# Decoder layer on one core: score operands projected already turned and read back from DRAM by pairs, and the feed-forward products of the first sequence put at the head of each attention step of the second

## What is computed

```python
q, k, v = split(x @ w_qkv)                      # 256 -> 3 x 256
q = q * cos + rotate_half(q) * sin              # the same for k
att = softmax(where(causal, q @ k.T * DH**-0.5, min))
x = layernorm(x + (att @ v) @ w_proj)
q = x @ Wq.T + bq; k = ctx @ Wk.T + bk; v = ctx @ Wv.T + bv
x = layernorm(x + softmax(where(mask, q @ k.T / 4, -inf)) @ v @ Wo.T + bo)
h = silu((x @ w1.T) * s1) * ((x @ w2.T) * s2)   # 256 -> 1024, ternary weights
h = gelu((h @ h1.T) * s3); h = gelu((h @ h2.T) * s4)   # 1024 -> 1024
x = layernorm(x + (h @ w3.T) * s5)              # 1024 -> 256
```

## Time and profile before

| | us |
|---|---|
| median of 3 runs | 994.16 |
| lowest and highest | 990.64, 994.91 |
| the profiled execution: its own time | 994.44 |
| the profiled execution: span of the instructions | 992.7 |
| busy in the span: TensorE (PE) | 869.8 |
| VectorE (DVE) | 559.3 |
| ScalarE (ACT) | 376.6 |
| GpSimd (POOL) | 363.5 |
| mean granted TensorE clock | 0.924 of full |

### The profile page before, as it was taken

The page is one execution under the profiler, slowest core; times in us unless marked ns, Lnnn a source line. Parts: engine busy times, 40 slices in busy tenths (PEclk is TensorE's granted clock), DMA queues, the critical chain, the costliest instruction groups (busy, mean ns, idle before and its releaser), DMA issues.

```text
span 992.7 us, 13083 instructions
## 1 busy us (share of the span) xinstructions
PE 869.8 (88%) x4466; PEld 553.7 (56%) x4466; DVE 559.3 (56%) x1422; ACT 376.6 (38%) x788; POOL 363.5 (37%) x575
## 2 busy tenths in 40 slices
PE   5879999797889877979999878889889869999997
PEld 2544444335725455645454435468765457888886
DVE  4697888777677654675565654342553476116213
ACT  0315665562453122224555664522343433112210
POOL 4312323546254332052222244252433375335433
PEclk9957999769867898979999989999999999999999
DMA  9909101002002111210101202133211126000000
GB/s 311 323 3 401 45 2 44 23 1 78 4 3 85 48 59 64 86 43 23 44 23 44 85 2 65 42 128 107 65 31 59 71 81 252 1 1 22 1 1 23
DMA packets 24955, 69.37 MB, mean 70 GB/s; under 512 B 4539, under 2 KB 12680, under 8 KB 24712
## 3 DMA queue, kind: packets, MB, share of 16 engines
q1 hardware_dynamic: 24888, 68.50, 20.1%
HBM read 65.87 MB, written 13.63 MB: 80 GB/s over the span
## 4 chain that ended last, share of the span: by engine, by line
PE 73%; DVE 12%; POOL 5%; ACT 5%; issue 3%; DMA 1%; SPq 0%; POOLq 0%; DVEq 0%; ACTq 0%
PE bank L880 13%; PE bank L946 11%; PE bank L684 8%; PE bank L701 7%; PE bank L649 5%; PE bank L635 3%; PE bank L584 3%; PE bank L867 3%; DVE bank L1300 3%; PE bank L928 2%; PE bank L823 2%; DVE max_raw L1298 2%; PE bank L811 2%; ACT prob_s L1103 2%; PE bank L734 1%
## 5 line engine op out<-in xcount | busy, mean ns | idle before, releaser
L1103 ACT ACTIVATE prob_s<-bank 128x512 f32<-128x512 f32 (+3 forms) x384 | 166.4, 494 | 131.3 <-PE bank L684 129.0
L1633 POOL TENSOR_SCALAR_AFFINE_SELECT prob_s<-prob_s 128x128 f32<-128x128 f32 x256 | 83.9, 343 | 178.4 <-ACT prob_s L1103 175.9
L1300 DVE CUSTOM_DVE_ANT_0 bank<-bank,causal_bf 128x128 f32<-128x128 f32 (+3 forms) x256 | 122.4, 511 | 46.0 <-PE bank L649 44.5
L649 PE MATMUL bank<-k_t_s,q_t_s 64*128 64x512 f32 (+3 forms) x384 | 135.6, 461 | 14.4 <-DVE max_raw L1300 11.3
L684 PE MATMUL bank<-q_t_s,k_t_s 64*128 64x512 f32 (+3 forms) x384 | 127.7, 431 | 21.5 <-ACT prob_s L1103 21.0
L684 PEld LDWEIGHTS bank<-q_t_s,k_t_s 64*128 64x128 f32 x384 | 61.5, 200 | 108.5 <-ACT prob_s L1103 64.4
L1298 DVE TENSOR_REDUCE max_raw<-bank 128x1 f32<-128x512 f32 x128 | 82.4, 685 | 51.9 <-PE bank L649 51.9
L880 PE MATMUL bank<-hid_f_hi_s,ring_s 128*128 128x512 f32 x256 | 105.7, 413 | 0.5 <-DVE qk_tok_s L1372 0.5
L880 PE MATMUL bank<-hid_f_lo_s,ring_s 128*128 128x512 f32 x256 | 104.2, 407 | 0.0
L946 PE MATMUL bank<-hid_hi_s,home_s 128*128 128x512 f32 x256 | 99.7, 390 | 0.0
L946 PE MATMUL bank<-hid_lo_s,home_s 128*128 128x512 f32 x256 | 99.7, 390 | 0.0
(11 more groups left out here) (156 smaller groups left out, 1523.7 us busy)
## 6 DMA issues: line engine op xcount, KB each, us to landing
ring_s<-scratch SPq DMA_DIRECT2D x44, 512.0 KB, 3.3
home_s<-scratch SPq DMA_DIRECT2D x22, 512.0 KB, 6.1
checked_s<-scratch SPq DMA_DIRECT2D x3, 3584.0 KB, 21.8
x_t_s<-in_x_t SPq DMA_DIRECT2D x2, 1024.0 KB, 5.6
x_tok_s<-in_x SPq DMA_DIRECT2D x2, 1024.0 KB, 5.9
out<-tok SPq DMA_DIRECT2D x16, 128.0 KB, 2.9
q_t_s<-max_rows SPq DMA_DIRECT2D x64, 4.0 KB
qx_t_s<-max_rows SPq DMA_DIRECT2D x64, 4.0 KB
```

What stands on the lines that cost most here:

```text
L649: mm(out[:, 0:k1 - k0], qkt(q, p, 0)[r, P * qt:P * (qt + 1)], qkt(q, p, 1)[r, k0:k1], start=True, stop=True).then_inc(S["max_mm"], 1)
L1103: act.activation(prob[q][4 * (s % 2) + j][:, 0:n], S_BANK[q][j][:, 0:n], ACT.Exp, scale=SCALE).then_inc(S["exp_done"], 1)
L1300: dve.tensor_tensor_reduce(out=out[:, 0:left], in0=out[:, 0:left], in1=L["causal_bf"][:, CHUNK - left:CHUNK], scale=1.0, scalar=NEG, op0=A ...
L1633: pool.affine_select(out=pr, in_=pr, compare_op=ALU.is_ge, fill=0.0, base=0, pattern=[[1, P]], channel_multiplier=-1).then_inc(S["select_d ...
```

## The change

1. q and k are projected with their columns on the partitions: `project_qk(q, g)` makes four groups g (i = g % 2: q or k; c = g // 2: which 512 tokens) of four 128x512 matmuls, `w_qkv` as the stationary operand. `rope` multiplies them by four tables of 512 KB each (before: two of 64 KB), POOL adds, ACT writes the hi part (`rope_hi`), DVE the lo part (`rope_lo`).
2. `keep_group` stores the parts to a DRAM tensor `scratch_qk` of [2, 8, 128, 1024] (1.5 MB per group), and `load_pair` reads a pair back: four DMAs per pair, each with a source of 8 slices (131,072 elements apart) of 8 rows, to 64 partitions; 1 MB per pair. A max unit waits for the load. `stage_hi`, `stage_lo`, `turn` and the copies of ACT are gone.
3. The same for the queries of cross attention: `project_q` makes four 128x128 products per 128 tokens instead of two of 128x256, `q_parts` writes the parts (three DVE instructions instead of one), `keep_queries` stores them in eight DMAs (3 MB), and `load_queries` reads them back in 16 DMAs, each of 256 KB with a source of 4 slices (262,144 elements apart) of 64 KB. `x_max` waits for the load. `x_turn` and its parts are gone.
4. Three constant 1 MB pieces are copied to these tensors at the start (`fill`). The copy of the feed-forward weights is moved from the start into SP's S steps (11 DMAs of 1 MB, steps -15 to -5), and the check loads to its steps -4 to 16, one each, all waiting for the whole copy.
5. FIRST_STEP is -15 instead of -20, there are 6 Q slots instead of 13, X steps start at -7 instead of -9.
6. In an attention step the F products come first. PLAN is shifted, and the layer h1 of chunk 0, done before score step 0 in the kernel before, now runs in steps -6 to 8 with a burst of eight Gelu activations of its own in step 9.

The diff, cut to its core:

```diff
-FIRST_STEP = stage_step(0)
+FIRST_STEP = max_step(0, 0)
...
 PLAN = [
-    (0, ("w1", "w2"), ("Q", 2), ("Q", 12), None, None),
-    (0, ("h1",), ("S", -18), ("S", -5), None, ("S", -4)),
-    (0, ("h2",), ("S", 0), ("S", 27), ("S", 29), ("S", 29)),
...
+    (0, ("w1", "w2"), ("Q", 4), ("S", -8), None, None),
+    (0, ("h1",), ("S", -6), ("S", 8), ("S", 9), ("S", 9)),
+    (0, ("h2",), ("S", 13), ("S", 27), ("S", 28), ("S", 28)),
...
+        def keep_group(q, g):
...
+            wait(sp, q, "rope_lo", 2 * (g + 1))
...
+        def load_pair(q, p, c, arrived):
+
+            for i in range(2):
+                for hh in range(2):
+                    sp.dma_start(qkt(q, p, i)[SLOT * hh:SLOT * (hh + 1), CHUNK * c[0]:CHUNK * c[1]].bitcast(F32),
+                                 a["scratch_qk"][i, :, DH // 2 * (2 * p + hh):DH // 2 * (2 * p + hh + 1), CHUNK * c[0]:CHUNK * c[1]]
+                                 ).then_inc(S[arrived], 16)
...
+        def load_queries(q):
+
+            wait(sp, q, "xq_out", 128)
+            wait(sp, q, "score_mm", 4 * LAST)
+            for p in range(NP):
+                for hh in range(2):
+                    h = 2 * p + hh
+                    sp.dma_start(qx_t[q][p][SLOT * hh:SLOT * (hh + 1), :].bitcast(F32),
+                                 a["scratch_x"][:, DH * h:DH * (h + 1), :]).then_inc(S[f"xq_in{p}"], 16)
...
-        for i, j in ((0, 4), (4, 12), (12, 20), (20, PIECES)):
-            sp.dma_start(a["scratch"][i:j], a["w_ffn"][i:j]).then_inc(L["scratch_in"], 16)
-
...
         for s in range(FIRST_STEP, S_END):
-            if s == rows_step(2):
-
-                sp.wait_ge(L["scratch_in"], 16 * 4)
-                for i in range(0, PIECES - 1, 7):
-                    sp.dma_start(checked[:, i:i + 7], a["scratch"][i:i + 7].rearrange("i p n -> p i n")).then_inc(L["check_in"], 16)
             attention(0, s)
...
+            n = s - FIRST_STEP
+            if n < PIECES // 2:
+
+                sp.dma_start(a["scratch"][2 * n:2 * n + 2], a["w_ffn"][2 * n:2 * n + 2]).then_inc(L["scratch_in"], 16)
+            n -= PIECES // 2
+            if 0 <= n < PIECES - 1:
+                sp.wait_ge(L["scratch_in"], 16 * (PIECES // 2))
+                sp.dma_start(checked[:, n], a["scratch"][n]).then_inc(L["check_in"], 16)
...
         def attention(q, s, slot=None, exact=True):
...
+            f_products(slot, exact)
             units = [(p, u) for p in range(NP) for u in range(NU) if max_step(p, u) == s]
...
-            f_products(slot, exact)
             norm_products(q, 0, s, ("yt", "proj"))
```

427 lines of the change are left out of this document (213 added, 214 removed), and 8 rows, old and new, of the table PLAN.

## The result

The changed kernel takes 1163.31 us (median of 4 runs, 1158.45 to 1164.64), the kernel before beside it 993.6 us (4 runs, 990.64 to 994.91): a ratio of 1.170, 95% interval 1.166 to 1.175. The forecast was 1095 with a range of 1030 to 1115, so the sign was right and the size was not. The profiled execution of after has a span of 1160.5 us, 167.8 more than the 992.7 of before.

What follows compares the result with a forecast made beforehand. DVE's reduces bound the score steps and lead-ins the rest, not busy TensorE. From 994.4 us: 38 + 31 + 12 + 2 - 9.5 + 17.7 + 8.4 + 1 = +100.6, so 1095, range 1030 to 1115.

Steps and rivals of the forecast that it cites:

- first cross attention: First sequence, last query part to first cross score: +31, from 25.6 to 57 us, with query reads at 103 GB/s.
- second lead-in: Second sequence, first projection to first score: -9.5, 115.5 us becoming 106; the max units come sooner, the first score later after them.
- first lead-in: Start to first score: +38, from 76.6 to 115 us; SP's wait for the weight copies holds pair 1's rows.
- transposes of score steps: Score steps: removing them gains 0, since windows with and without them took 14.09 and 14.07 us, under DVE's reduces.
- The rival in which TensorE is the path: Whole kernel: transposes cost their time, so removing 67.7 us of them makes it faster, near 960 us; chance 0.08.
- SP isn't held: First lead-in: the copies land early or SP reaches them sooner, so +13 instead of +38, total 1070; chance 0.13.
- the low rate of the reads: Read-backs from DRAM with few outer slices: 207 GB/s for pairs, 103 for queries, instead of the full 414.
- products put off: Second sequence's score steps: 77 products of layer h1 moved into steps 0 to 8 at 0.23 us each, +17.7.
- a second burst: Second sequence, step 9: a Gelu burst for layer h1, as step 29 already has, +8.4.
- case at full rate: All read-backs: they go at 414 GB/s, so first cross attention is +2 and the sum +48.6, 1043; chance 0.15.
- second cross attention: Second sequence's cross lead-in: +12, less than half of 31, as feed-forward products fill it though ring loads queue behind reads.
- products first: Attention steps with feed-forward products at the head: +1, bounds -3 and +8, as a max unit's bank is free anyway.

Runs made afterwards that it cites:

- ord: Changed kernel with only the check loads (which wait for the weight copies) moved behind the row DMAs of pair 1; 1160.45 us.
- late: Changed kernel with both the feed-forward weight copies and the check loads issued behind the row DMAs of pair 1; 1141.28 us.
- plan2: sum4 with the shifted feed-forward product table of the kernel before: h1 in steps -6 to -1 without burst, h2 over steps 1 to 27; 1053.15 us, ratio 1.0577 to before.
- sum4: Changed kernel with copies and check loads late, queries and pairs read at 128 partitions, and feed-forward products last in the step; 1064.75 us.
- plan1: Changed kernel with layer h1 of chunk 0 packed into steps -6 to -1, without the burst at step 9; 1165.88 us.
- queries_rows: Changed kernel with the queries' DRAM tensor laid out by heads, read by 64 rows in the first sequence and 128 in the second; 1127.25 us.
- sum4_ballast: sum4 plus 64 idle transposes per sequence at the old turn places of pairs 4 to 7; 1057.42 us, ratio 1.0595 to before.
- ballast: Changed kernel plus 64 idle transposes per sequence at the old turn places of pairs 4 to 7; 1156.19 us.
- flast: Changed kernel with the feed-forward products put back behind the scores and max units of an attention step; 1147.02 us.
- b_ffirst: Kernel before with feed-forward products leading each attention step of the second sequence, nothing else changed; 1005.45 us.

## Why the prediction was right and wrong

The sum missed by 67 us: 14.4 in the first cross attention, 15.4 in the second, 8.4 in the second lead-in and 12.7 in the score steps behind it, 8.7 in the score steps of the first sequence, 4.4 in the first lead-in, and 3 net in the small terms.

**Right: transposes of score steps lie in a shadow.** Doubling them made these steps 3.6 and 3.2 us longer for 17.4 us of work, and removing them shortened no stretch of score steps. The rival in which TensorE is the path (0.08) didn't come.

**Right in size, with the wrong cause first: first lead-in.** Forecast the first score at 115, measured 119.0. The forecast held that SP's wait for the copies holds the rows of pair 1. ord shows that without this wait the first score comes 2.7 us sooner at most; the rows stand behind 11 MB of copies all the same. That the number came near is luck in so far as the copies end both waits. The rival "SP isn't held" gave 89.6 for the first score if SP alone were freed; ord has 116.28, and only late, with the copies themselves moved, comes near it with 93.7.

**Right: the low rate of the reads.** A share of 0.25 and 94 GB/s in the reads of queries, forecast 0.25 and 100; in the pair loads 0.41 and 142, where 207 had been taken. One of its reasons was misread: the maxima aren't the only kind without a landing time in the list of before, the two masks of 77 KB have none either.

**Right in size by one pair of kernels: products put off, and a second burst.** 17.7 + 8.4 = 26.1 forecast, 27.7 by the steps of plan2 against those of sum4, which also differ in how h2 is spread. plan1, which takes both out of after and nothing else, has 14.4. The burst's own step is 8.2 us shorter without it, as priced; what a product costs in a step is not settled.

**Wrong: first cross attention, +31 for +45.4.** The failed step is "7 + 40.5 + 3.5 = 51", and then 57: between the stores and the rows it has the reads alone. The rate of the reads was right, but the eight loads for the second sequence, 3.6 MB, lie between them and the rows as well. They appear in the prediction only in its case at full rate, as part of "24 x 0.67". Measured, 6.2 us pass until the reads are issued (7), 50.3 until the rows are issued (40.5), and 14.5 until the first cross score (9.5), since two rounds of rows and their landings lie there. At 94 GB/s the reads alone would take 45 us, an estimate; SP was still issuing them for 28.35 and the loads for another 22. queries_rows measured what the reads are worth at a higher rate: 24.1 us of the 45.4.

**Wrong: second cross attention, +13 for +28.4.** "I take less than half", since products would fill the lead-in. That is the failed step. Products ran there, but on TensorE they stand in order behind max units that waited 24.8 us for the reads, and 13.3 for the rows, and no wait for a ring load is in the trace. In queries_rows, where only layout, stores and reads of the queries changed, the stretch is 85.0 us instead of 106.5, so 21.5 of the 28.4 go with the way of the reads.

**Wrong: score steps of the first sequence, 0 for +8.7.** The equal windows were both at a granted clock of 1.00. The failed step is the 0 for the transposes of score steps: it took the clock of the changed kernel for that of before. Measured, it is 0.78 in these steps after and 0.87 before, and the same steps 17 to 20 take 15.67 us at 0.78. What lowers it is not settled. Idle transposes at the old places brought it back in sum4_ballast (0.83, and 4 to 9.5 us), not in ballast. About 3 of the 8.7 may be spread between runs.

**Wrong: products first, +1 for 6 to 15.** The failed step is "a max unit's bank is free then anyway", from which the bounds were -3 and +8. The bank that counts is the products' own. flast gives 15.5 us: 9.0 in the second lead-in, which covers the 19.0 instead of 10.6 by which that stretch grew, and 9.5 in the score steps, less what comes back elsewhere. b_ffirst gives 11.0 against the profile of before and 5.8 against the execution beside it.

**Small terms.** From the second projection to the first max unit the forecast was -20.1, measured -23.8. For the query parts of the first sequence it was +1, measured +4.5; the granted clock there is 0.86 against 1.00 before, and that wasn't tried apart.

What stays open: of the 58 us by which plan2 is behind before, 14.3 lie ahead of the first score, 7 in the first sequence's steps, 20.5 from the last score to the first cross score of the first sequence, 10 in the second, and 6 in small pieces. In these a projection, its store and its read-back stand in a row, in the place of transposes that overlapped; how much of it a better order could hide was not tried.
